# Cross attention on one core: keys and queries as two 12-bit float32r parts in place of three bfloat16 parts, with the heads paired over the two 64-row halves of TensorE's array

## The reference, cut to what matters

```python
# x: (4, 256, 256); ctx_768: (4, 4096, 192); 16 heads of 16 columns
q = (layernorm(x) @ Wq + bq).reshape(B, Nq, H, D).transpose(0, 2, 1, 3)
k = (ctx_768 @ Wk + bk).reshape(B, Nkv, H, D).transpose(0, 2, 1, 3)
v = (ctx_768 @ Wv + bv).reshape(B, Nkv, H, D).transpose(0, 2, 1, 3)
attn = jnp.einsum('bhqd,bhkd->bhqk', q, k) * scale
attn = jnp.clip(attn, -CLAMP, CLAMP)
attn = jax.nn.softmax(attn, axis=-1)
x = jnp.einsum('bhqk,bhkd->bqhd', attn, v).reshape(B, Nq, Cq)
```

## Time and profile before

| | |
|---|---|
| runs shown | median 1134.89 us (1134.63 to 1138.36, 3 runs) |
| profiled execution, first to last instruction | 1137.6 us |
| PE / PEld busy | 1096.2 / 822.4 us |
| DVE busy | 854.9 us |
| ACT busy | 739.1 us |
| POOL busy | 441.2 us |
| DMA | 120.80 MB, mean 106 GB/s |

### The profile page before, as it was taken

How to read it: one execution, slowest core, us unless ns; L and a number is a source line. 1 busy time by engine, 2 the same in 40 slices (tenths; PEclk the granted TensorE clock), 3 DMA queues, 4 the chain that set the end, 5 groups by cost and what they waited for, 6 DMA issues and landing times.

```text
span 1137.6 us, 52429 instructions
## 1 busy us (share of the span) xinstructions
PE 1096.2 (96%) x22943; PEld 822.4 (72%) x22943; DVE 854.9 (75%) x1603; ACT 739.1 (65%) x1380; POOL 441.2 (39%) x759
## 2 busy tenths in 40 slices
PE   7999999999999999999999999999999998979997
PEld 6676677777777777878777777767778765646655
DVE  4777788888888888888888888879999723783642
ACT  2223777777777777777777777778878875414342
POOL 4456466464555555555555545213000001103220
PEclk9999999999999999999999999999999999998998
DMA  7767545454545445545444454423453010000001
GB/s 202 209 165 177 148 130 137 124 143 132 132 120 139 125 125 137 137 122 135 123 132 125 130 131 120 115 73 80 129 150 102 21 31 3 1 1 2 2 1 37
DMA packets 162884, 120.80 MB, mean 106 GB/s; under 512 B 19891, under 2 KB 161603, under 8 KB 162627
## 3 DMA queue, kind: packets, MB, share of 16 engines
q1 hardware_dynamic: 155619, 110.97, 36.4%
q10 hardware_dynamic: 7008, 6.23, 2.0%
HBM read 88.16 MB, written 28.84 MB: 103 GB/s over the span
## 4 chain that ended last, share of the span: by engine, by line
PE 88%; DVE 5%; ACT 3%; issue 1%; DMA 1%; SPq 0%; POOLq 0%; ACTq 0%
PE st L1529 19%; PE acc L1719 19%; PE mx L1529 18%; PE kps L1529 14%; PE st L1534 2%; DVE kst L1372 2%; PE misc L1529 2%; PE kps L1534 1%; PE mx L1534 1%; PE setB L1977 1%; ACT prob L1000 1%; PE acc L1534 1%; PE st L1891 1%; PE setA L2000 1%; DVE mxp L1115 1%
## 5 line engine op out<-in xcount | busy, mean ns | idle before, releaser
L1115 DVE TENSOR_REDUCE mxp<-mx 128x1 f32<-128x512 f32 x959 | 625.5, 686 | 141.1 <-PE mx L1529 114.0
L905 ACT ACTIVATE prob<-st 128x512 f32<-128x512 f32 x704 | 398.6, 599 | 132.5 <-PE st L1529 130.5
L1529 PE MATMUL st<-qst,kst 99*32 99x256 bf16 x8192 | 431.3, 272 | 1.9 <-ACT prob L905 1.1
L1529 PE MATMUL mx<-kst,qst 96*32 96x512 bf16 x3532 | 376.9, 380 | 1.2 <-DVE mxp L1115 0.2
L1529 PEld LDWEIGHTS st<-qst,kst 99*32 99x32 bf16 x8192 | 279.9, 97 | 85.0 <-ACT prob L905 5.0
L905 ACT ACTIVATE xn<-st 128x512 f32<-128x512 f32 x320 | 185.9, 599 | 61.0 <-PE st L1529 60.2
L1719 PE MATMUL acc<-prob,v_raw 128*17 128x256 f32 x2816 | 189.1, 378 | 1.4 <-ACT prob L905 1.2
L1529 PEld LDWEIGHTS mx<-kst,qst 96*32 96x32 bf16 x3532 | 125.3, 94 | 6.0 <-DVE mxp L1115 5.0
L1719 PEld LDWEIGHTS acc<-prob,v_raw 128*17 128x17 f32 x2816 | 99.0, 97 | 40.2 <-ACT prob L905 1.9
L1529 PE MATMUL kps<-xnT 128*32 128x256 bf16 x2088 | 94.3, 272 | 0.0
L640 POOL CAST xnT<-ctx 128x256 bf16<-128x256 f32 x87 | 34.4, 395 | 137.1 <-DMA ctx<-in_ctxT 84.4
(11 more groups left out here) (429 smaller groups left out, 1303.8 us busy)
## 6 DMA issues: line engine op xcount, KB each, us to landing
kst<-kscr SPq DMA_DIRECT2D x120, 192.0 KB, 3.0
kst<-kscr SPq DMA_DIRECT2D x360, 64.0 KB, 2.9
kscr<-kraw SPq DMA_DIRECT2D x100, 192.0 KB, 2.8
ctx<-in_ctxT SPq DMA_DIRECT2D x93, 128.0 KB, 2.7
ctx<-in_ctxT SPq DMA_DIRECT2D x180, 64.0 KB, 2.6
kscr<-prob SPq DMA_DIRECT2D x16, 192.0 KB, 3.7
kscr<-o_sb SPq DMA_DIRECT2D x12, 192.0 KB, 4.2
qscr<-v_raw SPq DMA_DIRECT2D x8, 192.0 KB, 2.5
```

The source lines that it names most:

```text
L905: act.activation(exps(n), st[n % 3][:, :], ACT.Exp).then_inc(exp_done, 1)
L1115: dve.reduce_max(at, bank_of_max(n)[:, :], AX.X).then_inc(max_red, 1)
L1529: mm = pe.matmul(to[32 * c:32 * c + 32, :], weights[:, 32 * c:32 * c + 32], moving, start=start, stop=stop, skip_group_check=True)
```

## The change

Keys and queries are kept as two parts of 12 significant bits in float32r, a 4-byte type. Three products of parts (first by first, second by first, first by second) make 48 rows; three rows carry the maximum in three parts. That makes `HR = 51` rows per head, in place of 99. Heads 0 and 2 of a group lie in partitions 0 to 50, heads 1 and 3 in 64 to 114.

A score unit is now two matmuls (`score_half`), each 51 rows by all 128 columns with 256 moving columns. A max unit is one matmul of 51 rows by 128 columns with 512 moving columns. It is issued between the two score halves, and it takes the head after the score unit's, so it lies in the other 64 rows of the array. The values and the projections keep their 32-column shapes.

The maxima's ring has three banks all along (`misc` is the third). Finished heads, lower bounds and turned maxima take their turns in the rings `st` and `mx`, worked out by the lists `mx_users` and `st_users`. Ahead of the main loop two max units are issued together, and then the filling of both. DVE no longer takes part in splitting keys: ACT copies the full number, POOL rounds it to the first part and subtracts. POOL also zeroes three rows of `qst` per half once in a head group. `values`, the projections and DVE's small steps are issued some units later or earlier than before.

```diff
-            def max_unit(product, n):
+            def max_unit(n):
...
-                wait(pe, max_red, n - 1 if n < NP + 2 else n - 2)
...
-                j, qt, at = m % 8 // 2, m % 2, n // 8 % RB * 512
-                product(bank_of_max(n)[:, :], qst[0:96, 4 * (q % 3) + j, qt * P:(qt + 1) * P],
-                        kst[0:96, j, at:at + 512], True, True).then_inc(max_ps, 1)
-
-            def score_unit(n):
+                mx_free(pe, "max", n)
+                j, qt, at = (m + 1) % 4, m % 8 // 4, n // 8 % RB * 512
+                row = slice(64 * (j % 2), 64 * (j % 2) + HR)
+                pe.matmul(bank_of_max(n)[:, :], qst[row, 2 * (q % 3) + j // 2, qt * P:(qt + 1) * P],
+                          kst[row, j // 2, at:at + 512], start=True, stop=True,
+                          skip_group_check=True).then_inc(max_ps, 1)
+
+            def score_half(n, h):
...
-                wait(pe, exp_done, n - 2)
...
-                for h in range(2):
-                    at = (8 * q + s // 2) % RB * 512 + (2 * s + h) % 4 * P
-                    mm = quarters(st[n % 3][:, h * T:(h + 1) * T], kst[0:99, j, at:at + P],
-                                  qst[0:99, 4 * (q % 3) + j, :], True, True)
-                mm.then_inc(st_ps, 1)
...
+                if h == 0:
+                    st_free(pe, "scores", n)
+                    if t == 0:
+                        pe.wait_ge(shift_set, 2 * q + 2)
+                at = (8 * q + s // 2) % RB * 512 + (2 * s + h) % 4 * P
+                row = slice(64 * (j % 2), 64 * (j % 2) + HR)
+                mm = pe.matmul(st_bank("scores", n)[:, h * T:(h + 1) * T], kst[row, j // 2, at:at + P],
+                               qst[row, 2 * (q % 3) + j // 2, :], start=True, stop=True, skip_group_check=True)
+                if h:
+                    mm.then_inc(st_ps, 1)
...
-                score_unit(n)
+                score_half(n, 0)
                 if n + AHEAD < NU:
-                    max_unit(quarters, n + AHEAD)
+                    max_unit(n + AHEAD)
+                score_half(n, 1)
...
-                if n >= 4 and t % 4 == 2:
-                    values((n - 4) // UQ, (n - 4) % UQ // 4)
...
+                if n >= 7 and t % 4 == 3:
+                    values((n - 7) // UQ, (n - 7) % UQ // 4)
...
-                if t % 8 in (0, 4):
+                if t % 8 in (1, 5):
                     g = t % 8 // 4
...
-            for n in range(AHEAD):
-                max_unit(whole, n)
-                f = fill(n)
...
+            for n in range(0, AHEAD, 2):
+                max_unit(n)
+                max_unit(n + 1)
+                filling(fill(n))
+                filling(fill(n + 1))
...
-                pool.wait_ge(k_r, k_steps(c + 1))
-                pool.tensor_copy(parts_of(c)[:, :, 1, :], kres[:, c % 2, :, :]).then_inc(k_2, 1)
-                pool.wait_ge(k_2, c + 1)
-                pool.tensor_tensor(parts_of(c)[:, :, 2, :], kres[:, c % 2, :, :], parts_of(c)[:, :, 1, :],
-                                   ALU.subtract).then_inc(k_3, 1)
+                full, first = parts_of(c)[:, :, 1, :], parts_of(c)[:, :, 0, :]
+                pool.wait_ge(k_full, k_steps(c + 1))
+                pool.tensor_copy(first.bitcast(F32R), full).then_inc(k_1, 1)
+                pool.wait_ge(k_1, c + 1)
+                pool.tensor_tensor(full, full, first, ALU.subtract).then_inc(k_2, 1)
...
-            def k_rest(c):
-
-                dve.wait_ge(k_1, c + 1)
-                wait(dve, k_3, c - 1)
-                dve.tensor_tensor(kres[:, c % 2, :, :], bank_of_k(c)[:, :].rearrange("p (g t) -> p g t", g=2),
-                                  parts_of(c)[:, :, 0, :], ALU.subtract).then_inc(k_r, 1)
```

More of the change, by code:

```diff
@@ L9 @@
 BF16 = mybir.dt.bfloat16
+F32R = mybir.dt.float32r
 I32 = mybir.dt.int32
@@ L30 @@
 AHEAD = UQ + LD
-NP = 11 * UQ + 48 + AHEAD
+HR = 51
 RB = 12
@@ L890, in _ @@
                 k_first(c)
-            for pair in range(2):
-                shift_rows(0, pair)
+            act.wait_ge(rows_set, 8)
+            shift_rows(0)
             k_first(KLEAD - 1)
```

417 lines of the change are left out of this document (220 added, 197 removed).

## The result

The changed kernel takes 1183.7 us in the median of four runs (1178.1 to 1191.4), the kernel before 1134.8. The ratio is 1.043, with a 95% interval from 1.038 to 1.049. I had forecast 1081, with 1036 to 1128 as range, so the sign was wrong too. The profiled execution has a span of 1177.2 us.

The account below looks back on a forecast made before the run. PE was taken as the bound, at 55.65 us a group in groups 1 to 10. The terms -47 - 7.5 - 4.5 - 3 + 2 + 6 = -54 gave 1134.9 - 54 = 1081 us, range 1036 to 1128.

Parts of the forecast that it names:

- Ahead of the main loop: Phase before the main loop: 38 max-unit pairs with shape changes cost +7, a shorter first chain gives about -1; +6 us.
- hidden: POOL's work, the DMAs and SP's earlier issue of the one-rows throughout the kernel: claimed to cost nothing.
- The change on PE: PE's units: 0.22 us each, one float32r column a cycle, 0.095 us per shape change, 0.107 per 128-column 4-byte first load.
- two cycles: Rival for all units: float32r streams at two cycles a column, 0.213 us more per unit, 1280 us; chance 0.09, including four cycles.
- stalled loads: Rival for max units: loads wait for the matmuls ahead to start, adding 0.107 us a unit, 1167 us; chance 0.07, either form.
- Groups 0 to 10: Main-loop groups with projections: 55.65 us a group falls to 51.4 with PE still the bound, -47 us for eleven.
- Group 11: Main-loop group with six half projections: 22 departures from the units and back, -14.5 + 7.0 = -7.5 us.
- Groups 12 to 14: Groups without projections: DVE sets the pace at 41.5 us in 12 and 13, -4.5 together, and -3 in 14.
- Coupling eats it: Rival for the main loop: PE waits 0.067 us a unit on DVE and ACT, nothing left, 1135 us; chance 0.04.
- Group 15: Group without maxima: cheaper score units -7, 28 departures from the units and back +9; +2 us.
- DVE's busy time: DVE over the kernel: busy time down by 55 to 60 us, with the keys' rest gone.

Follow-up runs that it names:

- e3: Changed kernel with only DVE's two clearings of query rows moved behind the layer norm; 1182.8 us.
- e16: Changed kernel with values in halves from group 11, earlier query load, clearings behind the norm, one-rows' transfers on POOL's queue, 12 and three filler matmuls; 1156.1 us.
- e8: e7 with half projections right behind `values` in the main loop, so bursts of four units; 1231.0 us.
- e10: e7 with the values of groups 12 to 14 in two halves, turned maxima behind the values and an earlier first query load; 1138.3 us.
- e7: Changed kernel with 31 fillers (identity matmuls) ahead of the first max unit; 1156.5 us.
- e2: Changed kernel, gap kept, with the first 76 max units each replaced by one whole-array bfloat16 identity product; 1144.6 us.
- e5: e2 with each stand-in in 51 rows of one 64-row half, two side by side; 1181.3 us.
- e6: Changed kernel with max units ahead of the main loop issued one at a time between the fillings, not in pairs; 1203.9 us.
- e11: Changed kernel, gap kept, with 24 identity matmuls over the whole array behind the tenth max unit; 1169.9 us.
- e1: Changed kernel with 22 identity matmuls (fillers) ahead of the first max unit; 1155.5 us.
- e15: Changed kernel with one-rows' transfers on ACT's queue and DVE's clearings behind the layer norm, without fillers; 1152.1 us.
- e9: e5 with each stand-in taking all 64 rows of its half; 1173.6 us.

## Why the prediction was wrong

**The step that failed: "Ahead of the main loop", +6 us.** It measured +45.2. I costed this phase at the full clock. Some 30 of the 45 are the clock (154.8 in the changed kernel, 124.9 and 125.0 with the gap filled). The rest, read from the kernel with 31 fillers, is 5.9 for the later first max unit (4.5 of it in the changed kernel, 1.4 the fillers' own), where I had set -1, and 9.4 for the phase, where I had set +7. I wrote "PEclk is 1.00 throughout" of the main loop and did not look at the dip ahead of it. The kernel before idled 2.33 us at that place and ran at half clock for 3.4. The trace had the warning; the change made the wait longer and put shapes behind it in which the clock does not come back.

The later first max unit is a second miss in the same step, from things that I had called hidden. "SP issues the one-rows earlier, in front of the first key's write, whose data are later anyway" was wrong: the transfers hold up what stands behind them. The DVE clearings delay the layer norm by 3 us. Taking away the clearings alone brought nothing (e3); both together, with the load ahead of the third key chunk's write, brought 3.0 us (e16). Most of the 4.5 us lies between the query's write and the first max unit (14.3 us for 10.65). There, too, I had put the DMAs at nothing, and no run shows which part of them it is. The transfers alone on a queue of their own were not tried.

**The change on PE: right.** One record per max unit, 0.23 us a unit for 0.22, a load under a running matmul of its own half, 0.095 us a change of shape and 0.107 a first load. Float32r streams one column a cycle: with 512 columns in each half a unit takes 0.23 us, and one column a cycle is 0.213. The rivals of two cycles and of stalled loads are out.

**Groups 0 to 10: -47 us forecast, -12.5 measured.** In size this is nearly as large a miss as the first one. In groups 1 to 10 a group is 54.6 us, where I had 51.4: 1.1 us less than before, not 4.3. Two terms are wrong. From one `values` to the next there are 3.22 us for 3.38, which saves 2.6 us in sixteen of them, where 14.1 - 10.2 = 3.9 was forecast; the unit's size (0.23 for 0.22) makes 0.6 of the difference, and 0.7 is not assigned. Another 1.7 us come at three or four places of a group, where lower bounds, a finished head or the turned maxima stand between units. On top of the ordinary cycles these places took 1.6 us before. I had set 1.2, and they take 2.9. PE's new idle time (534.33 busy of 545.70, 1.1 us a group) is part of it; moving the turn took back 0.4. Group 11 gave 2.3 in place of 7.5; with values in halves it gives 5.1.

**Groups 12 to 14: wrong.** Forecast -7.5, measured +5.6 and +3.7. I took DVE's work as the pace. The rival "Coupling eats it" had the wait: PE is idle 0.08 us a unit in groups 12 and 13 (82.75 busy of 93.10), where 0.067 takes the whole gain. The argument against it failed: "a burst of two needs two of three banks" holds where projections cut the bursts. I did not carry it to groups 12 to 14, where they are four. e8 and e10 show it from both sides. Group 15 was +4.8 for +2, and with halves +7.4.

**DVE's busy time** fell by 38.7 us, not by 55 to 60. The keys' rest is gone as forecast (38.0 in groups 1 to 10), but the same 640 reductions there are busy 430.6 us in place of 417.4, since fewer of them follow each other closely.

**The sum of the rest.** Had the clock stayed up, the forecast would still have missed: e7 has 1156.5.

## What to carry to other kernels

Ahead of a change, read the clock in every stretch where PE idles, not only in the busiest one. A dip that costs 2 us now can cost 30 when the work behind it changes, as e2 and e5 show. Check rings by the longest run of units between two other blocks, not by the mean rate; cutting a block in two can be worth more than the changes of shape that it adds (groups 12 to 14), or less (group 15). Measure a group up to its last unit. And before crediting a repaired version, give the old kernel the same repair: here that took the whole lead.

## What the runs showed of the hardware

**The clock's level persists.** With PE fully busy the granted clock stayed at the 1.2 GHz level for 75 us (more than 84 in e6) when blocks of whole-array matmuls alternated with products in one or both 64-row halves. It came back within 5 us when the same blocks alternated with whole-array products (e2), or in a stretch of them in a row (e11). From the 2.4 GHz level the same alternation kept 2.4 GHz (e1, e7, e15). The Trainium skill ("TensorE: Matmul & The Clock Gate", Part 1) says that idleness halves the clock and that sustained activity restores it. The traces agree on the first (2.33 and 4.54 us of idle time, while 1.85 in e1 and 1.99 in e16 left the profiled runs at full). On the second they agree in e2 and e11 and not in the 75 us.

It is not changes of shape as such. At the start of the main loop the changed kernel fell to half again, and came back within 7 us, with PE full and its units alternating with 17- and 32-column shapes:

```profile
157.00:164.00 7.00, 7.00 (x52) 3.71 (x52) 3.77 (x6) 3.85 (x8) 1.46 (x3) 0.51 1.04 340
164.00:170.00 6.00, 6.00 (x80) 3.49 (x84) 4.42 (x7) 3.78 (x8) 2.70 (x5) 1.00 0.40 114
```

So what e2, e5 and e9 show holds for half-array products between whole-array blocks. Why these keep the clock down, and what let it rise at 109 us, no run isolates.

**Transfers onto three partitions.** The four one-row transfers (276 KB in all) moved at about 27 GB/s in a stretch with next to no other traffic (11.8 to 14.5 us of the changed kernel), and on POOL's queue they took 8 to 10 us to land.
